# One stacked product for the attention scores, and weight splits in another order, in a fused LSTM, attention, GRU and expert kernel

## What is computed

```python
q = einsum('bld,dhk->blhk', h, Wq);  latent = einsum('bld,dc->blc', h, Wkv_down)
k = einsum('blc,chk->blhk', latent, Wk_up);  v = einsum('blc,chk->blhk', latent, Wv_up)
attn = softmax(where(causal, einsum('bqhd,bkhd->bhqk', q, k) / sqrt(64), -inf))
y = einsum('bqhd,hdo->bqo', einsum('bhqk,bkhd->bqhd', attn, v), Wout)
x = x + y                                      # h: the LSTM's states
x = x + experts(gru(x, cond, ...), gate_w, w1, b1, w2, b2)
```

## Time and profile before

| | us |
|---|---|
| median of three runs | 558.43 |
| lowest and highest | 557.41, 561.45 |
| the profiled execution | 559.31 |
| its span in the profile | 557.4 |
| TensorE, weight loads, VectorE, ScalarE, GpSimd busy | 521.5, 480.1, 420.2, 347.8, 32.2 |

### The profile page before, as it was taken

How to read it: one execution, slowest core, us unless ns; L and a number is a source line. 1 busy time by engine, 2 the same in 40 slices (tenths; PEclk the granted TensorE clock), 3 DMA queues, 4 the chain that set the end, 5 groups by cost and what they waited for, 6 DMA issues and landing times.

```text
span 557.4 us, 20232 instructions
## 1 busy us (share of the span) xinstructions
PE 521.5 (94%) x7376; PEld 480.1 (86%) x7418; DVE 420.2 (75%) x2338; ACT 347.8 (62%) x1297; POOL 32.2 (6%) x85
## 2 busy tenths in 40 slices
PE   8979888899789999999999999999999999989998
PEld 3746676789779999999999999999999998889997
DVE  4536787869877888888888888888989797864442
ACT  2224454677357676767676767776767767666662
POOL 7000000000000000000000000000000000000000
PEclk9689969799959999999999999999999999999999
DMA  8910101001010101010101010101101010100000
GB/s 211 351 11 11 16 6 14 11 7 16 13 15 5 19 3 21 13 20 3 21 14 19 4 19 15 17 8 13 15 15 15 8 15 15 18 2 1 13 6 11
DMA packets 75118, 14.32 MB, mean 26 GB/s; under 512 B 71411, under 2 KB 74111, under 8 KB 74638
## 3 DMA queue, kind: packets, MB, share of 16 engines
q1 hardware_dynamic: 74566, 11.96, 11.8%
q10 hardware_dynamic: 456, 1.08, 0.6%
HBM read 7.78 MB, written 1.05 MB: 16 GB/s over the span
## 4 chain that ended last, share of the span: by engine, by line
PE 75%; DVE 15%; ACT 4%; issue 4%; DMA 1%; SPq 1%; POOL 0%; ACTq 0%; DVEq 0%; POOLq 0%
PE pH L488 21%; PE pY L488 12%; PE pG L488 12%; PE pL L488 9%; PE pV L488 8%; PE pC L580 6%; PE pC L488 4%; PE pS L488 4%; DVE latNlo L990 2%; DVE mx L996 1%; DVE acc L1085 1%; ACT hid L872 1%; DVE ghi L1164 1%; DVE gB L1161 1%; DVE glo L1167 1%
## 5 line engine op out<-in xcount | busy, mean ns | idle before, releaser
L872 ACT ACTIVATE hid<-pH,b 128x256 f32<-128x256 f32 (+1 forms) x320 | 114.8, 438 | 4.9 <-PE pH L488 4.9
L488 PE MATMUL pY<-w,hid 128*128 128x128 f32 x608 | 84.2, 281 | 0.0
L488 PE MATMUL pH<-ghi,w1hi 128*128 128x256 f16 (+1 forms) x320 | 75.9, 253 | 3.1 <-ACT hid L872 1.6
L488 PE MATMUL pH<-glo,w1hi 128*128 128x256 f16 (+1 forms) x320 | 76.0, 254 | 0.0
L488 PE MATMUL pH<-ghi,w1lo 128*128 128x256 f16 (+1 forms) x320 | 75.9, 254 | 0.0
L488 PEld LDWEIGHTS pY<-w,hid 128*128 128x128 f32 x608 | 73.7, 191 | 0.2
L879 ACT ACTIVATE gT<-pG 128x32 f32<-128x32 f32 x128 | 24.6, 192 | 68.2 <-PE pG L488 68.2
L1139 DVE SCALAR_TENSOR_TENSOR gRZ<-gT,g 128x32 f32<-128x32 f32 x128 | 24.4, 190 | 39.2 <-ACT gT L879 37.9
L910 ACT ACTIVATE lC<-lT 128x16 f32<-128x16 f32 x128 | 28.0, 219 | 39.0 <-DVE lT L1176 38.7
L580 PE MATMUL pC<-ident,P 128*128 128x128 f32 x256 | 43.2, 294 | 6.4 <-DVE acc L1085 4.6
L897 ACT ACTIVATE lT<-pL 128x64 f32<-128x64 f32 x128 | 28.8, 225 | 32.1 <-PE pL L488 22.4
(11 more groups left out here) (181 smaller groups left out, 1619.5 us busy)
## 6 DMA issues: line engine op xcount, KB each, us to landing
w<-in_w SPq DMA_DIRECT2D x2, 2048.0 KB, 13.0
qbd<-qh SPq DMA_DIRECT2D x256, 16.0 KB, 1.9
out<-acc SPq DMA_DIRECT2D x16, 64.0 KB, 1.5
xT<-in_xT ACTq DMA_DIRECT2D x1, 960.0 KB, 7.7
hid<-in_WqT SPq DMA_DIRECT2D x1, 512.0 KB, 5.3
hid<-in_Wout SPq DMA_DIRECT2D x1, 512.0 KB, 9.9
lWh<-in_lWh SPq DMA_DIRECT2D x1, 256.0 KB, 2.8
lWx<-in_lWx SPq DMA_DIRECT2D x1, 256.0 KB, 3.1
```

The source lines that it names most:

```text
L488: return nc.tensor.matmul(o, lhsT=lhsT, rhs=rhs, start=start, stop=stop, skip_group_check=True)
L872: A(hid[:, e % NHID, c, 0:W], pH[half][:, W * at:W * (at + 1)], ACT.Gelu, bias=b1[:, e, c:c + 1], scale=1.0 / SP).then_inc(gelu, 1)
```

## The change

- The three products of a sequence become one. The queries of a period are spread once into qst: rows 0 to 31 the high part, 32 to 63 the high part again, 64 to 95 the low part. Beside it latst holds on the same rows the high, the low, and the high part of the latents. The product over 96 rows is the sum of the three. A sequence's 128 columns (head and query) stand in qst 16 elements apart.
- `spread_queries` runs once a period: 4 DMAs for each of the three groups of rows, the first eight wait for q_hi alone. The memset of qbd goes.
- GpSimd writes latst, in two instructions between lathi and latlo. `scores` waits for these and for all twelve DMAs.
- qh is stored in the order in which the queries come out of TensorE, in `q_copy` and `q_rest`.
- The splits of w1 and b2 stand in other steps (tables W1_HI, W1_LO, B2_HI, B2_LO), the scaling of two GRU weights in steps 5 and 8, and w1 has its own semaphore.
- keep_warm: two more products before the transposes in steps 18 to 29, two fewer at the end of step 23.

```diff
-W1_STEP = (17, 18, 19, 20, 21, 22, 23, 25)
+W1_HI = {17: (0,), 18: (1,), 19: (2, 3), 24: (4,), 25: (5,), 26: (6,), 27: (7,)}
+W1_LO = {18: (0,), 19: (1, 2), 24: (3, 4), 26: (5, 6), 27: (7,)}
+B2_HI = {9: (0, 0), 10: (0, 1), 11: (64, 0), 16: (64, 1), 17: (96, 0), 25: (96, 1)}
+B2_LO = {10: (64, 0), 11: (64, 1), 12: (96, 0), 17: (96, 1)}
...
-        qh = sb("qh", [128, 2, B, 2, HG, TB], f16)
-        qbd = sb("qbd", [128, 2, 4, 2, HQ, 32], f16)
+        latst = sb("latst", [3 * LD, B, T], f16)
+        qh = sb("qh", [128, 2, 2, HG * TB * B], f16)
+        qst = sb("qst", [3 * LD, 2, H * TB, B], f16)
...
-            def spread_queries(n):
-                p, u = divmod(n, NU)
-                if u == 0:
-                    sp.wait_ge(q_lo, p + 1)
-                if n == 0:
-                    sp.wait_ge(cleared, NCLEAR)
-                if n >= 2:
-                    sp.wait_ge(s_mm, n - 1)
-                for q in range(HQ):
-                    r = slice(32 * q, 32 * q + 32)
-                    sp.dma_start(qbd[r, n % 2, :, :, q, :].rearrange("p j l c -> p (j l) c"),
-                                 qh[r, p % 2, 4 * u:4 * u + 4, :, :, :].rearrange("p b l g t -> p (b l) (g t)")).then_inc(qbd_done[n % 2], 16)
+            def spread_queries(p):
+                for r, (l, ready) in enumerate(((0, q_hi), (0, q_hi), (1, q_lo))):
+                    sp.wait_ge(ready, p + 1)
+                    if p >= 2 and r == 0:
+                        sp.wait_ge(s_mm, NU * (p - 1))
+                    for q in range(HQ):
+                        sp.dma_start(qst[LD * r:LD * (r + 1), p % 2, 32 * q:32 * q + 32, :].rearrange("p c b -> p (c b)"),
+                                     qh[32 * q:32 * q + 32, p % 2, l, :]).then_inc(qst_done[p % 2], 16)
...
                 pool.wait_ge(lat_split, 2 * G + 1)
+                pool.tensor_copy(latst[:, :, c], lathi[0:96, :, c]).then_inc(lat_stack, 1)
+                pool.wait_ge(lat_stack, 2 * G + 1)
+                pool.tensor_tensor(latst[32:64, :, c], latT[32:64, :, c], lathi[32:64, :, c], ALU.subtract).then_inc(lat_stack, 1)
+                pool.wait_ge(lat_stack, 2 * G + 2)
...
-                pe.wait_ge(lat_split, 2 * (p + 1))
-                pe.wait_ge(qbd_done[n % 2], 16 * HQ * (n // 2 + 1))
+                pe.wait_ge(lat_stack, 2 * (p + 1))
+                pe.wait_ge(qst_done[p % 2], 16 * 3 * HQ * (p // 2 + 1))
...
-                    S = S4[:, j, :]
-                    mm(S, flat(qbd[:, n % 2, j, 0, :, :]), lathi[:, b, 0:L])
-                    mm(S, flat(qbd[:, n % 2, j, 0, :, :]), latlo[:, b, 0:L])
-                    last = mm(S, flat(qbd[:, n % 2, j, 1, :, :]), lathi[:, b, 0:L])
+                    last = mm(S4[:, j, :], qst[:, p % 2, :, b], latst[:, b, 0:L])
...
                 if unit_at(k, O_T) is not None:
+                    if LAG <= k < WARM_END:
+                        keep_warm(k, 2)
                     turn_probs(unit_at(k, O_T), k)
...
-                if k < WARM_END:
+                if k < WARM_END and not (LAG <= k and t % GS == GS - 1):
                     keep_warm(k, startup_fill(k))
...
-                if k in W1_STEP:
-                    e = W1_STEP.index(k)
-                    act.wait_ge(loaded_moe, 4 * 16)
+                for e in W1_HI.get(k, ()):
+                    act.wait_ge(loaded_w1, 16)
                     A(w1hi[:, e, :], w1[:, e, :], ACT.Copy, scale=SW).then_inc(set_w1hi, 1)
```

More of the change, by code:

```diff
@@ L330, in build @@
         q_lo = sem("q_lo")
-        qbd_done = [sem(f"qbd_done{n}") for n in range(2)]
+        qst_done = [sem(f"qst_done{n}") for n in range(2)]
         s_mm = sem("s_mm")
@@ L364, in build @@
         HALVES = (0.5, 1.0)
-        NCLEAR = 12
+        NCLEAR = 11
         PARTS = (0, 64, 96)
@@ L399, in _ @@
                 sp.dma_start(b2[q:q + 1, :], a["b2"].rearrange("(o e) d -> o (e d)", o=1)).then_inc(loaded_b2, 16)
[L400 removed]
+            sp.dma_start(whole(w1), a["w1"]).then_inc(loaded_w1, 16)
+            for t, name in ((tri, "tri"), (b1, "b1"), (w2, "w2")):
                 sp.dma_start(whole(t), a[name]).then_inc(loaded_moe, 16)
[L403 to L414 removed]
+            def spread_queries(p):
[6 more added lines that the diff above has]
+                                     qh[32 * q:32 * q + 32, p % 2, l, :]).then_inc(qst_done[p % 2], 16)
             def store(i):
@@ L422, in _ @@
             for k in range(STEPS + 2):
[L423 to L427, removed]
+                if latents_at(k - 1) is not None:
+                    spread_queries(latents_at(k - 1))
                 for i in range(NG):
@@ L818, in setup @@
                     A(gWhi[:, :, :], gW2[:, 0:2, :], ACT.Copy).then_inc(set_gru, 1)
-                if k in (26, 27):
-                    c = slice(512 * (k - 26), 512 * (k - 25))
-                    act.wait_ge(loaded_b2, 3 * 16)
-                    A(b2P[:, c], b2[:, c], ACT.Copy).then_inc(set_b2, 1)
-                if k in (28, 29):
-                    c = slice(512 * (k - 28), 512 * (k - 27))
-                    act.wait_ge(set_b2lo, k - 27)
-                    A(b2P[64:128, c], b2[64:128, c], ACT.Copy).then_inc(set_b2, 1)
-                if k in (30, 31):
-                    c = slice(512 * (k - 30), 512 * (k - 29))
-                    act.wait_ge(set_b2lo, k - 27)
-                    A(b2P[96:128, c], b2[96:128, c], ACT.Copy).then_inc(set_b2, 1)
-                if k in W1_STEP:
-                    e = W1_STEP.index(k)
-                    act.wait_ge(loaded_moe, 4 * 16)
+                if k in B2_HI:
+                    q, half = B2_HI[k]
+                    c = slice(512 * half, 512 * (half + 1))
+                    if q == 0:
+                        act.wait_ge(loaded_b2, 3 * 16)
+                    else:
+                        act.wait_ge(set_b2lo, PARTS[1:].index(q) * 2 + half + 1)
+                    A(b2P[q:128, c], b2[q:128, c], ACT.Copy).then_inc(set_b2, 1)
+                for e in W1_HI.get(k, ()):
+                    act.wait_ge(loaded_w1, 16)
                     A(w1hi[:, e, :], w1[:, e, :], ACT.Copy, scale=SW).then_inc(set_w1hi, 1)
@@ L841, in q_copy @@
                 if p >= 2:
-                    for half in range(2):
-                        act.wait_ge(qbd_done[half], 16 * HQ * NU // 2 * (p - 1))
-                A(qh[:, p % 2, :, 0, :, :], pC[:, :].rearrange("p (g s b) -> p b g s", g=HG, b=B),
-                  ACT.Copy, scale=1.0 / SP).then_inc(q_hi, 1)
+                    act.wait_ge(qst_done[p % 2], 16 * 3 * HQ * (p // 2))
+                A(qh[:, p % 2, 0, :], pC[:, :], ACT.Copy, scale=1.0 / SP).then_inc(q_hi, 1)
             def exps(n):
@@ L1110, in setup_late @@
             def setup_late(k):
-                if k in (27, 28):
-                    c = slice(512 * (k - 27), 512 * (k - 26))
-                    dve.wait_ge(set_b2, k - 26)
-                    V.tensor_tensor(b2[64:128, c], b2[64:128, c], b2P[64:128, c], ALU.subtract).then_inc(set_b2lo, 1)
-                if k in (29, 30):
-                    c = slice(512 * (k - 29), 512 * (k - 28))
-                    dve.wait_ge(set_b2, k - 26)
-                    V.tensor_tensor(b2[96:128, c], b2[96:128, c], b2P[96:128, c], ALU.subtract).then_inc(set_b2lo, 1)
-                if k - 1 in W1_STEP:
-                    e = W1_STEP.index(k - 1)
+                if k in B2_LO:
+                    q, half = B2_LO[k]
+                    c = slice(512 * half, 512 * (half + 1))
+                    dve.wait_ge(set_b2, (PARTS.index(q) - 1) * 2 + half + 1)
+                    V.tensor_tensor(b2[q:128, c], b2[q:128, c], b2P[q:128, c], ALU.subtract).then_inc(set_b2lo, 1)
+                for e in W1_LO.get(k, ()):
                     dve.wait_ge(set_w1hi, e + 1)
```

15 lines of the change are left out of this document (7 added, 8 removed).

## The result

The changed kernel takes 613.59 us (median; 611.98 to 615.6), the kernel before 558.3 us beside it. The ratio is 1.0971, 95% interval 1.094 to 1.1003: 55.3 us slower. I had said 552.0 us, and 543 to 567.

A forecast was written before the change was run, and what follows sets the result against it. TensorE's queue of matmuls was taken to bound the kernel, VectorE's chain in places. Gains 1.8 + 2.1 + 1.0 + 0.35 + 1.5 = 6.75 us from the profiled 559.3 gave 552.5, from the median 551.6; forecast 552.0 us, range 543 to 567.

The forecast's parts named there:

- The spreads: Twelve query DMAs before unit 0, one per 0.36 us: landed after 5.6 us, 0.7 us before needed, so no wait.
- rival A: The twelve query DMAs come late for unit 0, from a pace of 0.42 us: 562 or 592 us; chance 0.15.
- All three signs: Signs of being wrong: qst wait every period, its weight loads well over 0.1 us, granted clock under 1.00 after 170 us.
- Rival C: Lighter scoring steps let one or two more 10 us stretches fall to 1.2 GHz: 557 to 560 us; chance 0.10.
- Units 0 and 2: Scores before steps 3 and 5 of every eight: fewer products save 1.8 and 2.1 us, together between 0 and 8.8.
- units 1 and 3: Scores before steps 4 and 6 of every eight: nothing won, bound by VectorE's chain and ScalarE's g.
- rival B: Strided weight loads of the scores are slow, 0.191 us each: 563 us, halfway 557; chance 0.10.
- the two rules: Strided query weights: SBUF line crossings cost part or all of 3.9 us, or the fast load reads strided at no loss.
- GpSimd: "Hidden": Two more GpSimd instructions a period ahead of latlo, each bounded by 0.441 us: latents about 0.9 us later, hidden.
- The splits: Weight splits in another order on VectorE's chain: 3.5 added, 4 removed, 0.35 us won; bounds 2 us lost or won.
- The fills: Clock-keeping products in steps 20 to 23, 28 and 29: 1.5 us won, from 6 won to 6 lost.
- first wait: TensorE's 3.62 us wait for queries in the first period: 1.0 us less, bounds 0 and 1.5.

## Why the prediction was wrong, step by step

- **The spreads: the step that failed.** "With 0.32 us and a gap of 0.04 the last of twelve starts 11 x 0.36 = 4.0 us after the first", and so "I take no wait". The pace is 0.67 us. The durations came from issues that touch DRAM; between two places in SBUF an issue takes 0.59 to 0.64 us in every shape tried, and the one row that had this, the old spreads at 0.65 us, I set aside for its 256 pieces. Even from DRAM the new shape took 0.43 us, already the turning point. The mechanism was there as rival A, with its turning point of 0.42 us, a price of 592 us at 0.65 and a chance of 0.15, but my range of 543 to 567 left that price out. It measured 42.9 us of wait behind the first period (38 in the rival) and 5.5 us in the first, where I had promised 1.0 us less than 3.62. All three signs that I had named for being wrong came: the wait in every period, weight loads at 0.164 us, and a clock under 1.00 after 170 us.
- **What rival A lacked: the clock.** It priced the wait alone. The falls of the clock with these waits are 10.4 us more, which was in no case of mine as a consequence. Rival C looked for its cause in the thin scores, and that is refuted.
- **Units 0 and 2: right in place and size, lost elsewhere.** I forecast 1.8 and 2.1 us; the step lengths show 2.4 and 2.4, and for units 1 and 3, where I had nothing, 0.4 more and 1.0 less. The strided loads (rival B) are there, 0.164 us a load, but cost 1.7 us and not the 11 of the rival: packed, the median step of unit 0 falls from 3.16 to 3.03 us, and the next one, which the prediction had on VectorE's chain, grows from 3.91 to 4.03. Of the two rules that the prediction set against each other, the one by which a stride costs is borne out by the load itself.
- **GpSimd: "Hidden", wrong, 5 to 6 us.** I looked for who reads the latents, and nobody waits for them. The price is paid by who computes beside them: 0.33 to 0.39 us in thirteen of the periods, on VectorE's chain. No rival had it.
- **The splits: right in sign, mis-sized.** 0.35 us forecast, about 2 measured, inside my bounds. **The fills: 1.5 us forecast, none measured.** The stretch at 67 to 85 us did come up from 0.72 to 1.00, but it is at 0.91 with the splits alone, and no time followed from fills.

Added up from 558.3 us: splits 2 less, units 0 and 2 4.8 less, GpSimd 5.0 more, waits 42.9 more, first wait 1.9 more, clock 10.4 more: 611.7, where 613.6 were measured. The 1.9 us between I can't place; single terms from different kernels needn't add.

## What to carry to other kernels

Price a DMA's issue by a row with the same two ends (SBUF or DRAM) and not by its shape alone, multiply by all that stand in the queue ahead of the wait, and where the forecast hangs on one pace with a known turning point, weigh both sides of it by the nearest row of the same kind. A wait that comes back every period (here 2.3 to 4.1 us) can cost its length and a stretch at the lower clock with it. And work moved to GpSimd "off the path" can still lengthen VectorE's instructions beside it: look at what runs there at the same time, above all short ones with both inputs in SBUF, and put it beside those that read PSUM.

## What the runs showed of the hardware that I had not expected

- An issue on SyncE's queue takes 0.59 to 0.64 us from SBUF to SBUF for 4, 32 or 128 rows, and 0.43 us from DRAM for 32 or 128. GpSimd's issue of the same copy took 0.498 us, and 0.651 us with 512 pieces of 64 bytes.
- A load of 96x128 weights takes 0.164 us at a stride of 32 bytes and 0.096 us packed; four products in a row can't hide it.
- gB and g, begun beside an instruction of GpSimd, ended 0.03 us behind it, up to 0.24 us late; x1T, which reads PSUM, did not.
- Twelve DMAs of 512 small pieces, on two queues, landed after 3.2 us at the median, where four on one queue landed after 2.1.
